# DLRM tower on one core: ten fields instead of eight looked up by one-hot products, each one-hot in one VectorE instruction

## The reference

```
e = jnp.stack([tbl_0[ids[:, 0]], ..., tbl_25[ids[:, 25]]], axis=1)
combined = jnp.concatenate([dense_features[:, None, :], e], axis=1)
interactions = jnp.einsum('bfd,bgd->bfg', combined, combined)
z = jnp.concatenate([dense_features, interactions[:, iu, ju]], axis=1)
h = jnp.concatenate([z, dense_features], axis=1)
h = jnp.maximum(h @ W_top1 + b_top1, 0.0)     # 607 -> 512
h = jnp.maximum(h @ W_top2 + b_top2, 0.0)     # 512 -> 256
y = h @ W_top3                                 # 256 -> 1
```

## Time and profile before

| | us |
|---|---|
| median of 3 runs | 406.57 (405.83 to 408.05) |
| profiled execution | 407.14 |
| its span, first to last instruction | 405.3 |
| GpSimd busy | 276.2 |
| TensorE busy | 321.7 |
| VectorE busy | 220.4 |
| ScalarE busy | 135.6 |

### The profile page before, as it was taken

One profiled execution on the slowest core, in us unless ns is written; L12 is line 12 of the kernel. 1 busy time (PEld: TensorE's weight loads), 2 busy tenths in 40 slices (PEclk: granted clock), 3 DMA queues, 4 the chain that ended last, 5 costly groups with the idle time before them and its releaser, 6 DMA issues.

```text
span 405.3 us, 14215 instructions
## 1 busy us (share of the span) xinstructions
PE 321.7 (79%) x6049; PEld 297.7 (73%) x6049; DVE 220.4 (54%) x684; ACT 135.6 (33%) x265; POOL 276.2 (68%) x292
## 2 busy tenths in 40 slices
PE   0566669859999799895999599996999699968556
PEld 0456568748988689885988499885988589858456
DVE  1799558914595637734395526835395527702123
ACT  2254323224233524341433324341434324332202
POOL 5777777777777777777777777777777777771000
PEclk9999989998999989996999979996999889996958
DMA  7966824682267115631257115641357115320320
GB/s 206 208 199 171 225 61 115 138 202 59 56 133 200 54 52 115 195 77 52 65 136 188 52 52 113 192 89 52 64 146 177 52 52 117 108 55 21 52 57 1
DMA packets 41518, 44.15 MB, mean 109 GB/s; under 512 B 29268, under 2 KB 34396, under 8 KB 40494
## 3 DMA queue, kind: packets, MB, share of 16 engines
q1 hardware_dynamic: 32278, 24.91, 25.8%
q0 software_dynamic: 9216, 18.89, 17.4%
HBM read 38.12 MB, written 5.65 MB: 108 GB/s over the span
## 4 chain that ended last, share of the span: by engine, by line
POOL 49%; issue 18%; PE 16%; DVE 7%; DMA 5%; SPq 2%; ACT 1%; POOLq 0%; ACTq 0%; DVEq 0%
POOL rows L259 49%; PE ps_o L286 5%; DVE onehot L619 4%; PE ps_g L311 3%; PE ps_m L325 3%; DMA h<-small_tables 3%; DVE tbl_lo L610 2%; DMA rows<-tables,idx 2%; SPq L213 2%; PE ps_t L297 2%; PE ps_o L369 1%; DMA x<-interaction_scratch 1%; PE ps_m L352 1%; PE ps_t L369 1%; PE ps_g L382 1%
## 5 line engine op out<-in xcount | busy, mean ns | idle before, releaser
L259 POOL DMA_INDIRECT rows<-tables,idx x288 | 276.0, 958 | 90.2 <-issue 86.3
L619 DVE TENSOR_SCALAR onehot<-oh_ids,rownum 125x256 fp32r<-125x256 int32 x512 | 159.6, 384 | 103.6 <-PE ps_o L286 66.7
L286 PE MATMUL ps_o<-onehot,tbl_hi 125*128 125x256 f32 x512 | 139.8, 307 | 31.6 <-DMA ident<-identity 14.9
L286 PE MATMUL ps_o<-onehot,tbl_lo 125*128 125x256 f32 x512 | 134.1, 296 | 0.4 <-issue 0.4
L286 PEld LDWEIGHTS ps_o<-onehot,tbl_hi 125*128 125x128 f32 x512 | 104.9, 205 | 39.0 <-DMA ident<-identity 14.9
L286 PEld LDWEIGHTS ps_o<-onehot,tbl_lo 125*128 125x128 f32 x512 | 105.2, 205 | 0.6 <-issue 0.6
L486 ACT ACTIVATE emb<-ps_o 128x256 f32<-128x256 f32 x64 | 38.4, 717 | 84.4 <-PE ps_o L286 84.4
L297 PE MATMUL ps_t<-ident,rows 128*128 128x128 f32 x288 | 46.3, 292 | 23.3 <-DMA rows<-tables,idx 23.2
L311 PE MATMUL ps_g<-emb 128*32 128x27 f32 x4096 | 54.9, 198 | 12.2 <-issue 5.9
L495 ACT ACTIVATE emb<-ps_t 128x512 f32<-128x512 f32 (+1 forms) x80 | 50.9, 664 | 37.2 <-PE ps_t L297 36.7
L311 PEld LDWEIGHTS ps_g<-emb 128*32 128x32 f32 x4096 | 46.3, 112 | 23.1 <-issue 16.0
(11 more groups left out here) (53 smaller groups left out, 211.8 us busy)
## 6 DMA issues: line engine op xcount, KB each, us to landing
oh_ids<-onehot_ids SPq DMA_DIRECT2D x8, 896.0 KB
rows<-tables,idx POOLq DMA_INDIRECT x288
interaction_scratch<-inter SPq DMA_DIRECT2D x32, 91.0 KB
x<-interaction_scratch SPq DMA_DIRECT2D x24, 117.0 KB
interaction_scratch<-inter SPq DMA_DIRECT2D x32, 81.2 KB
x<-small_tables SPq DMA_DIRECT2D x4, 448.0 KB
h<-small_tables SPq DMA_DIRECT2D x4, 448.0 KB
dense<-dense_t SPq DMA_DIRECT2D x8, 128.0 KB
```

What stands on the lines that cost most here:

```text
L259: pool.indirect_dma_start(rows[h][:, k, :], None, tables[k], bass.IndirectOffsetOnAxis(ap=idx[:, NG * (2 * i + h) + k:NG * (2 * i + h) + k ...
L286: mm = pe.matmul(o, tbl[p][:, k, c, :], onehot[k % 2][:, c, :], start=(c + p == 0), stop=(c == TCHUNKS - 1 and p == 1))
L619: op = nc.vector.tensor_scalar(onehot[k % 2][:, c, :], oh_ids[:, k, :], rownum[:, c:c + 1], None, ALU.is_equal)
```

## The change

It has these parts.

- Two more fields of 1000 rows, 21 and 22, go from the gathers to the one-hot lookups: 16 gathered fields in four groups of four, 256 gathers, and ten looked up.
- The one-hot of a field is made by one `tensor_tensor` of 125 x 8 x 256 elements. Both inputs are tensors: the ids repeated over the 8 chunks, the row numbers repeated over the 256 samples.
- Three one-hot buffers instead of two. VectorE makes fields 0 to 2 of the next block in advance, where it was 0 to 3.
- ScalarE makes the rounded part of `x` and of the first layer's output (a second ReLU from PSUM); VectorE keeps the subtractions.
- The tables are staged through four buffers instead of two at the start; the ids of a block are loaded in two parts.
- The chip's loop is written out: all 8 blocks stand in the program. TensorE's order in a block is lookups in pairs, with a group of the first half's transposes behind each of the first four pairs; then layer 1; the gram products of the first half; the second half's transposes; layer 2; the gram products of the second half; layer 3.
- Layer 3 multiplies the other way round (result 1x256) and each block's result is stored at once; the transpose at the end goes.
- In the last block one band of stores and one load of `x` are issued by ScalarE.
- The memory for the descriptors of indirect transfers is set to 4096 bytes per partition, where it was at its default.

```diff
-ONEHOT = [3, 7, 9, 10, 11, 13, 15, 17]
+ONEHOT = [3, 7, 9, 10, 11, 13, 15, 17, 21, 22]
...
-        onehot = [sb(f"onehot{s}", [TPART, TCHUNKS, BLOCK], f32r) for s in range(2)]
+        onehot = [sb(f"onehot{s}", [TPART, TCHUNKS, BLOCK], f32r) for s in range(SLOTS_OH)]
...
-                wait(dve, onehot_used, NO * i + (k - 1 if k else 0))
-                for c in range(TCHUNKS):
-                    op = nc.vector.tensor_scalar(onehot[k % 2][:, c, :], oh_ids[:, k, :],
-                                                 rownum[:, c:c + 1], None, ALU.is_equal)
+                wait(dve, onehot_used, n - SLOTS_OH + 1)
+                ids = oh_ids[0:TPART, k, :].unsqueeze(1).to_broadcast([TPART, TCHUNKS, BLOCK])
+                numbers = rownum[:, :].unsqueeze(2).to_broadcast([TPART, TCHUNKS, BLOCK])
+                op = nc.vector.tensor_tensor(onehot[n % SLOTS_OH][:, :, :], ids, numbers, ALU.is_equal)
...
+            def body(i):
+                a, b, m = 2 * i, 2 * i + 1, i - 1
+                for u in range(NU):
+                    lookup(i, 2 * u)
+                    lookup(i, 2 * u + 1)
+                    if u < NGR:
+                        transposes(a, u)
+                for n in range(K1):
+                    layer1(m, n)
+                grams(a)
+                for g in range(NGR - 1):
+                    transposes(b, g)
+                layer2(m, 0)
+                transposes(b, NGR - 1)
+                layer2(m, 1)
+                grams(b)
+                layer3(m)
...
+            def last_relus():
+                store_band(act, LAST, 1)
+                load_x(act, LAST, 2)
+                split_x_hi(LAST)
...
-    nc = bacc.Bacc("TRN2", target_bir_lowering=False, num_devices=1)
+    nc = bacc.Bacc("TRN2", target_bir_lowering=False, num_devices=1, dynamic_dma_scratch_size=4096)
```

More of the change, by code:

```diff
@@ L243, in _ @@
-            with sp.Fori(1, BLOCKS - 1) as i:
-                next_block_loads(i)
-                turn_interactions(i)
-            turn_interactions(BLOCKS - 1)
-            sp.wait_ge(y_row, 1)
-            sp.dma_start(out, yrow[:, :]).then_inc(out_stored, 16)
-            sp.wait_ge(out_stored, 16)
+            for n in range(4, NO):
+                load_stage(n)
+            load_dense(1)
+            load_ids(1, 0)
+            for n in range(NO, ITEMS):
+                load_stage(n)
@@ new lines, in _ @@
+            load_ids(1, 1)
+            for i in range(1, BLOCKS):
+                turn_interactions(i - 1)
+                if i < LAST:
+                    load_ids(i + 1, 0)
+                    load_dense(i + 1)
+                    load_ids(i + 1, 1)
+                if i >= 2:
+                    store_y(i - 2)
+            load_x_dense(LAST)
+            store_band(sp, LAST, 0)
+            load_x(sp, LAST, 0)
+            load_x(sp, LAST, 1)
+            store_y(LAST - 1)
+            store_y(LAST)
@@ L290, in transposes, with lookup @@
-            def transposes(i, h, g):
-                s, n = GROUPS[g]
-                q = NGR * h + g
-                pe.wait_ge(gathered[h][g], 16 * n * (i + 1))
-                wait(pe, rows_placed, 2 * NGR * i + q - 1)
+            def lookup(i, k):
+                n, u = NO * i + k, NU * i + k // 2
+                if i == 0:
+                    pe.wait_ge(stage_split, k + 1)
+                pe.wait_ge(onehot_ready, n + 1)
+                if k % 2 == 0:
+                    wait(pe, onehot_placed, 2 * (u - 1))
+                o = ps_o[u % 2][:, BLOCK * (k % 2):BLOCK * (k % 2 + 1)]
+                for c in range(TCHUNKS):
+                    for p in range(2):
+                        mm = pe.matmul(o, tbl[p][:, k, c, :], onehot[n % SLOTS_OH][:, c, :],
+                                       start=(c + p == 0), stop=(c == TCHUNKS - 1 and p == 1))
+                mm.then_inc(onehot_used, 1)
@@ L451, in _ @@
             pe.wait_ge(ident_loaded, 16)
-            body(0, first=True)
+            first_body()
             pe.wait_ge(w3_biases_loaded, 16 * 3)
-            with pe.Fori(1, BLOCKS - 1) as i:
+            for i in range(1, BLOCKS):
                 body(i)
-            body(BLOCKS - 1, last=True)
-            pe.wait_ge(y_copied, BLOCKS - 1)
-            layer3(BLOCKS - 1)
-            pe.wait_ge(y_copied, BLOCKS)
-            pe.transpose(ps_t[0][0:2 * BLOCKS, 0:128], ycol[:, :], ident[:, :]).then_inc(y_turned, 1)
+            last_layer1([PAIR_CHUNKS])
@@ L678, in body @@
-            def body(i, last=False):
-                make_onehot(i, 4)
+            split_lo(NO + 1)
+            make_onehot(NO + 1)
+            add_dense_weights()
+            make_onehot(NO + 2)
+            split_lo(DENSE_ITEM)
+            split_lo(DENSE_ITEM + 1)
+            for i in range(1, BLOCKS):
+                n = NO * i
+                make_onehot(n + 3)
+                if i > 1:
+                    copy_y(i - 2)
+                make_onehot(n + 4)
                 place_dense(i)
@@ L700, in _ @@
[L700 to L709 removed]
+                    make_onehot(n + k)
+                split_x_lo(i - 1)
```

626 lines of the change are left out of this document (270 added, 356 removed).

## The result

The median went from 406.77 us (4 runs) to 497.5 us (4 runs, 495.29 to 501.09): 1.2247 times the time before, interval 1.219 to 1.2303. The profiled execution took 499.42 us for a span of 497.6. The direction was forecast, and so was the place; the size was 40 us short of what was measured.

What follows compares the result with a forecast made beforehand. GpSimd's unbroken issue of gathers was taken as the bound: last gather at 326.4 us, plus 96 of stalls and 33.6 of tail, gives a 456 us span, forecast 457 us; mechanism bounds 434 to 486, range 412 to 500.

Steps and rivals of the forecast that it cites:

- What bounds the kernel: GpSimd issues gathers without a break, 1.25 us apart, the last ending at 366.7 us; TensorE is near this limit.
- Gathers, 32 fewer: On GpSimd: 256 gathers instead of 288, at 1.248 us each, take 40 us off its chain.
- What it does to the gathers: 80 two-input one-hots on VectorE hold back GpSimd's gathers, 1.2 us each, 96 us in all, bounds 72 to 124.
- a gather gets in at each seam: Where one-hots follow directly on VectorE, one gather starts between two of them, every 2.25 us: 1.0 us lost each.
- More than one seam is lost: Rival: gathers get no turn between VectorE instructions, or both engines take turns; 2.0 to 2.17 us per one-hot, 522-536 us; 6%.
- The one-hot instruction: On VectorE: one two-input instruction of 125x2048 takes 2.3 us, where eight narrow ones took about 2.5.
- Lookups: On TensorE: two more per block add 3.5 us net, 40.3 becoming 43.8 or 43 us a block; hidden behind GpSimd.
- first rival: The wide one-hot doesn't hold gathers, so TensorE is last at 43 us a block: 386 to 388 us; 14%.
- Descriptor space: For GpSimd's gathers: 4096 bytes costs nothing if two gathers in flight fit; taken as nothing.
- Casts to ScalarE, third buffer: Casts moved off VectorE hide in ScalarE's idle time; the extra one-hot buffer gains nothing while GpSimd is last.
- Tail: Behind the last gather: stores split over two queues and no result transpose, 38.6 becomes 33.6 us.
- VectorE at half rate: Rival: mixed types slow the one-hot to 4.5 us per field, VectorE becomes the bound, over 600 us; 2%.

Runs made afterwards that it cites:

- a_scalar_first: The changed kernel with one-hots by eight one-input instructions and the result's and dense copies first in a block, ahead of the fourth one-hot: 402.18 us, 0.9861 times before.
- a_y_moved: The changed kernel with only VectorE's copy of the result moved behind the tenth one-hot of a block: 459.37 us.
- a_copies_moved: The changed kernel with the copy of the result and the two dense-column copies moved behind the tenth one-hot: 456.67 us, 1.1232 times before.
- b_tensor: The kernel before with each one-hot by one instruction with two input tensors instead of eight with one: 493.38 us, 1.2046 times before.
- after: The changed kernel itself, with all parts of the change, against the kernel before: 497.5 us, 1.2247 times before.
- a_scalar_moved: The changed kernel with one-hots by eight one-input instructions and all three copies behind the tenth one-hot: 402.39 us, 0.9882 times before.
- a_spare_copy: a_y_moved with a spare one-partition copy of the same size, SBUF to SBUF, in the old place of the result's copy: 495.03 us.
- a_dense_moved: The changed kernel with only the two copies of the dense column moved behind the tenth one-hot: 492.81 us.
- a_onebank: The changed kernel with one PSUM bank for the transposes instead of two, nothing else; the control for a_psum: 501.86 us.
- a_psum: The changed kernel with the one-hot's row numbers in a PSUM bank given up by the transposes, so one input is in SBUF: 415.24 us, 1.0186 times before.
- a_scalar: The changed kernel with each one-hot again by eight instructions with one input tensor, copies left in place: 417.53 us median of nine runs; ratio 1.0082.

## Why the prediction was right in direction and short in size

The measured 497.5 us lie outside 434 to 486, the bounds that the prediction gave its own mechanism, and inside its range of 412 to 500 by 2.5 us. The range was drawn so wide to part the rivals, not from a reason to expect 138 us of stretch, so that it holds the result is partly luck.

- *What bounds the kernel*: right. GpSimd's gathers are the chain before and after.
- *Gathers, 32 fewer*: right in count. The gain was covered by the stretch; `a_scalar_first`, where the last gather ends 22 us earlier than before and 18.8 us of waits for TensorE lie ahead of it, shows it.
- *What it does to the gathers*: the mechanism was right, and the step that failed is "a gather gets in at each seam". The term of 96 us measured 142 - 4 = 138. The seams admit a gather except in a run with a single-partition copy directly ahead, and there it stays out for 5 or 6 one-hots. `a_y_moved`, which takes that away, has a stretch of 103 us in all, where 96 + 4 were forecast, and at 459.4 us it comes 2 us from the forecast of 457; `a_copies_moved` hits it term by term (stretch 100, last gather at 423.4 us where 422.4 was forecast), and its mean gather of 1338 ns is the 1.3 us named as a sign. The average price of a one-hot, 1.2 us, was near: 1.28 in `a_y_moved`, 1.45 in `b_tensor`.
- The profile before couldn't show it: the copies of a result there (128 partitions, 149 ns on average) are followed by a pause of 0.6 to 0.8 us in all six middle blocks, and no single-partition copy stands ahead of a run of one-hots. But the prediction named the case, under *More than one seam is lost*, and gave it 3% for the whole program (half of that rival's 6%). What it lacked is a version of it for a part of the program: six runs of six one-hots that lose 2.1 instead of 1.0 us each come to 40 us, and `after` has 142.4 - 102.6 = 40 us more of stretch than `a_y_moved`.
- *The one-hot instruction*: 2.3 us forecast, 2.28 measured.
- *Lookups*: 43 us a block were too few: the gram products stand 45.7 us apart in `a_scalar_moved` and 45.1 in `a_scalar_first`. It made no difference to the forecast, but to its first rival: seven blocks of 2.1 to 2.7 more put 387 at 402 to 406, and `a_scalar_first` has 402.
- *Descriptor space*, at nothing: right in the kernel before (0.9992).
- *Casts to ScalarE, third buffer*, at nothing: ScalarE is busy 167.2 us and has 1% of the chain; no run took them apart.
- *Tail*: 33.6 forecast, 32.5 measured.
- Last gather's end: 422.4 forecast, 465.05 measured, 42.6 late, which is the whole error of the span (456 against 497.6) but for 1.1 us of tail.
- *The rivals*: what the rule of exclusive turns would do (VectorE waiting too) didn't come, since the one-hot kept its duration; VectorE at half rate neither. That GpSimd loses every seam came in part, as said above.

## What to carry to other kernels

Where GpSimd's gathers set the end, price a VectorE instruction by what it does to them, not by its own duration: the wide one with two SBUF inputs kept VectorE busy 11 us less than the narrow ones in the same program (179.8 and 190.8 us) and stretched the gathers by 142 us instead of 55. One input in PSUM took the waiting away here (gathers at 983 ns), and so did the narrow form with a scalar per partition once the copies stood elsewhere (964). And look at what stands directly ahead of a long unbroken run on VectorE: a copy of 0.4 us there cost 38 us more than the same copy behind the run.

## What the runs showed of the hardware that I had not expected

- A gather that missed the first seam behind a short single-partition copy missed all the seams between the one-hots that followed, up to 12.55 us, in all 24 runs of one-hots of the wide form with both inputs in SBUF (six each in `after`, `a_spare_copy`, `a_dense_moved` and `a_onebank`). There each one-hot overlapped the next by 0.069 to 0.072 us, in the runs of `a_copies_moved` and `a_y_moved`, which admit gathers, by 0.074 to 0.087. With one input in PSUM (`a_psum`) the overlap behind the copy is just as short, and gathers get in. How far into the one-hot the gather starts doesn't decide: one that started 0.867 us in missed its seam behind the copy, others of 0.867 to 0.869, in runs without the copy, were admitted. Why the copy does it is open.
- It happens with one-input instructions too (13.4 us in `a_scalar`), where a gather otherwise waits for nothing: VectorE gives way instead, one of its instructions of 0.335 us then taking 0.545.
- Every wait that ended at a seam ended 0.12 to 0.13 us before the VectorE instruction did, over the 193 gathers of more than 1.2 us in `after`, `a_copies_moved` and `a_spare_copy` (one ended 0.113 us before).
